# One block for mixing and output: first loads spread over the mixing, transposes that read V in place

## What is computed

```
xn = layernorm(x)
# branch 1: projection to v and two controls, twice a long causal convolution and a gate, output projection
proj = xn @ in_proj_w + in_proj_b
for i in range(2):
    h = implicit_filter(2048, ...)          # one filter a channel, with an exponential window
    v = fft_conv(v, h) * gated_control(ctrl[i], ...)
attn = v @ out_proj_w + out_proj_b
# branch 2
h = bitlinear(xn, w_fc) + gate * (xn @ v.T @ fast_b.T @ u.T)
ffn = bitlinear(relu(h) ** 2, w_proj)
return x + attn + ffn
```

## Time and profile before

| | |
|---|---|
| runs of the kernel, median (lowest to highest) | 952.39 us (951.21 to 956.0) |
| the profiled execution: its time, its span | 950.16 us, 948.6 us |
| TensorE matmul, busy share of the span | 90% |
| TensorE weight load | 76% |
| VectorE, ScalarE, GpSimd | 67%, 50%, 26% |
| moved by DMA | 152.84 MB, mean 161 GB/s |
| granted TensorE clock, mean | 0.963 |

### The profile page before, as it was taken

How to read it: one execution, slowest core, us unless ns; L and a number is a source line. 1 busy time by engine, 2 the same in 40 slices (tenths; PEclk the granted TensorE clock), 3 DMA queues, 4 the chain that set the end, 5 groups by cost and what they waited for, 6 DMA issues and landing times.

```text
span 948.6 us, 26467 instructions
## 1 busy us (share of the span) xinstructions
PE 858.3 (90%) x9972; PEld 716.5 (76%) x9973; DVE 633.6 (67%) x1025; ACT 478.9 (50%) x678; POOL 250.1 (26%) x267
## 2 busy tenths in 40 slices
PE   6836999999999964999999999999999999993995
PEld 3325878888888853888888888888888888873885
DVE  6973898998989972455556565555656556553885
ACT  6413777777777772344443443434334344334761
POOL 1023665646646501111121121211112112110111
PEclk9968999999999996999999999999999999995999
DMA  5373224233242138676778868777777777696797
GB/s 180 105 233 130 94 89 170 97 122 143 88 155 111 73 108 283 123 174 155 166 144 195 182 154 170 148 178 174 171 156 159 177 167 166 125 191 145 241 337 264
DMA packets 86705, 152.84 MB, mean 161 GB/s; under 512 B 12981, under 2 KB 62278, under 8 KB 85382
## 3 DMA queue, kind: packets, MB, share of 16 engines
q1 hardware_dynamic: 74902, 109.01, 47.6%
q0 software_dynamic: 11472, 41.69, 13.4%
q10 hardware_dynamic: 288, 1.57, 0.5%
HBM read 102.83 MB, written 49.41 MB: 160 GB/s over the span
## 4 chain that ended last, share of the span: by engine, by line
PE 47%; DVE 4%; DMA 4%; issue 3%; ACT 2%; SPq 0%; ACTq 0%; POOL 0%; POOLq 0%; DVEq 0%
PE py L1081 14%; PE pp L1062 13%; PE pf L410 6%; PE pf L411 6%; PE pf L412 6%; DVE r L959 2%; DMA Tmid<-filters 1%; DVE r_lo L964 1%; DMA xf_hbm<-xb 1%; DMA GC<-xf_hbm 1%; DMA out<-GC 1%; PE po L410 1%; PE pyT L1273 1%; ACT yg_hi L1207 1%; PE po L411 1%
## 5 line engine op out<-in xcount | busy, mean ns | idle before, releaser
L1081 PEld LDWEIGHTS py<-vwin,lead 64*64 64x64 f32 x5120 | 134.2, 134 | 36.6 <-issue 36.6
L1011 ACT ACTIVATE r_hi<-r 128x512 fp32r<-128x512 f32 x128 | 80.8, 631 | 159.8 <-DVE r L959 159.8
L1081 PE MATMUL py<-vwin,lead 64*64 64x128 f32 (+4 forms) x5120 | 148.1, 266 | 13.7 <-issue 13.5
L964 DVE TENSOR_TENSOR r_lo<-r,r_hi 128x512 fp32r<-128x512 f32 x128 | 101.5, 793 | 78.8 <-ACT r_hi L1011 78.8
L1008 ACT ACTIVATE r<-pf 128x512 f32<-128x512 f32 x128 | 76.6, 598 | 131.9 <-PE pf L412 126.9
L1062 PE MATMUL pp<-wproj,r_hi 128*128 128x256 f32 x512 | 135.7, 298 | 3.6 <-DVE r_lo L964 1.9
L1062 PE MATMUL pp<-wproj,r_lo 128*128 128x256 f32 x512 | 127.2, 281 | 0.0
L451 POOL TENSOR_SCALAR lead<-lead,norms 128x256 f32<-128x256 f32 x64 | 115.3, 1813 | 3.4 <-POOL norms L445 3.4
L1062 PEld LDWEIGHTS pp<-wproj,r_hi 128*128 128x128 f32 x512 | 96.7, 189 | 20.1 <-DVE r_lo L964 6.1
L611 DVE SCALAR_TENSOR_TENSOR xc<-ctrl,taps,xc 128x512 f32<-128x512 f32 x128 | 97.2, 778 | 18.8 <-ACT xc L683 18.1
L959 DVE TENSOR_TENSOR r<-r 128x512 f32<-128x512 f32 x128 | 101.6, 794 | 4.9 <-ACT r L1008 0.6
(11 more groups left out here) (158 smaller groups left out, 1602.7 us busy)
## 6 DMA issues: line engine op xcount, KB each, us to landing
lead<-filters SPq DMA_DIRECT2D x128, 320.0 KB, 6.0
xnT_hbm<-split_b SPq DMA_DIRECT2D x32, 512.0 KB, 3.1
tokens<-xnT_hbm POOLq DMA_DIRECT2D x32, 512.0 KB, 6.9
lead<-in_attn_x SPq DMA_DIRECT2D x16, 512.0 KB, 3.8
gc_hbm<-xc SPq DMA_DIRECT2D x16, 512.0 KB, 2.7
xb<-in_attn_x POOLq DMA_DIRECT2D x16, 512.0 KB, 7.3
GC<-gc_hbm SPq DMA_DIRECT2D x32, 256.0 KB, 7.0
GC<-xf_hbm SPq DMA_DIRECT2D x16, 512.0 KB, 6.7
```

Of the source, the lines that this page charges most:

```text
L964: dve.tensor_tensor(r_lo[j][:, :], r[j][:, :], r_hi[j][:, :].bitcast(F32), ALU.subtract).then_inc(r_split, 1)
L1011: act.activation(r_hi[j][:, :], r[j][:, :], ACT.Copy).then_inc(r_hi_done, 1)
L1081: last = pe.matmul(py[g % 2][q * BW:(q + 1) * BW, side, l, :, A:NB], tile[rows, q * PAIR + l, j * BW:(j + 1) * BW], vwin[g % 2][rows, q, l ...
```

## The change

`output_stage` is gone as a block; its work stands at the end of `mix_stage`, in the same block, without a barrier. Five things change with it:

- The first loads of the output are spread. In order 1, SP's program has its iterations written out; the output weights are loaded after iteration 0, and the gates and the sum of chunks 0 to 3 after iterations 1 to 4. The split of the output weights (`wo_hi`, `wo_lo`) is made within the last iteration of the mixing.
- The transposes read V itself as stationary operand, with a step of 512 bytes from one element to the next. The copies into `ys` are gone, and so are the waits on them.
- The results go to other memory: the transposes to `py`, the output matmuls to `pf` and `pp` in turn, `yg` to a part of GC1's room, the split parts to the feed-forward weights' room, `wo`'s parts to the tokens' room.
- The first two chunks are started between the last feed-forward tiles.
- TensorE's program for the 16 chunks is written out instead of looping.

The core of the diff:

```diff
+                for m in range(ITERS):
+                    body(m, m + ITERS, False)
+                    if m == 0:
+                        sp.wait_ge(y_out, GROUPS // ORDERS + 2)
+                        load_wo(sp)
+                    elif m <= SLOTS:
+                        load_gates(sp, m - 1, m - 1)
+                        sp.wait_ge(xf_saved, 16 * m)
+                        load_sum(sp, m - 1, m - 1)
...
-            sp.wait_ge(y_out, GROUPS // ORDERS + 2)
-            sp.wait_ge(xf_saved, 16 * SLOTS)
-            load_output(sp)
...
+                for c in (SLOTS, SLOTS + 1):
+                    gates(c, c % SLOTS)
+                sp.wait_ge(xf_saved, 16 * (NCH - 1))
...
+            def output(c, j):
+                gated(c, j)
+                summed(c - 2, (j + 2) % SLOTS)
+                yg_low(c, j)
...
+            gated(0, 0)
+            low(NCH - 1, HT - 1)
+            yg_low(0, 0)
+            gated(1, 1)
             scale(NCH - 1)
             add(NCH - 1)
+            yg_low(1, 1)
+            for c in (2, 3):
+                output(c, c)
...
+                    if last and order == ORDERS - 1 and g == 0:
+                        act.wait_ge(wo_in, 16 * KT)
+                        act.wait_ge(fc_mm, (NCH - 1) * HT + HT)
+                        act.activation(wos[0][:, :, :], wo, ACT.Copy).then_inc(wo_hi_ready, 1)
...
+            act.wait_ge(fc_mm, NCH * HT + HT)
+            high(0, 0)
+            high(1, 1)
             act.wait_ge(xf_ready, NCH + 1)
             act.dma_start(xf_hbm[NCH - 1], xb[:, :, :]).then_inc(last_saved, 16)
...
             def transposed(c, j):
                 i = j % 2
-                pe.wait_ge(ys_ready, c + 1)
                 pe.wait_ge(yg_ready, c + 1)
                 for t in range(TB):
-                    last = pe.transpose(pT[i][:, t, :, :].rearrange("p k j -> p (k j)"), ys[i][:, t, :], ident[:, :])
+                    last = pe.transpose(pT[i][:, t, :, :].rearrange("p k j -> p (k j)"), V[:, :, c // CPB, (c % CPB) * TB + t], ident[:, :])
                 last.then_inc(yT_mm, 1)
...
+                pe.wait_ge(y_out, GROUPS + 2)
+                transposed(0, 0)
+                proj(NCH - 1, HT - 2)
+                transposed(1, 1)
+                proj(NCH - 1, HT - 1)
+                pe.wait_ge(wo_split, 1)
+                pe.wait_ge(relu_done, NCH * HT + 2)
+                projected(0, 0)
+                pe.wait_ge(xf_ready, NCH + 1)
+                for c in range(2, NCH):
+                    transposed(c, c % SLOTS)
+                    projected(c - 1, (c - 1) % SLOTS)
+                projected(NCH - 1, (NCH - 1) % SLOTS)
```

More of the change, by code:

```diff
@@ L854, in mix_stage, with lagging @@
         Gs = GC1[:, :, :, :].rearrange("p (b c) n a -> p b c (n a)", b=SIDES)
-        def lagging(eng, order, body):
+        def lagging(eng, order, body, closing=False):
             if order == 0:
                 body(0, 0, True)
-            with eng.Fori(1 - order, ITERS) as m:
+            end = ITERS - (closing and order == ORDERS - 1)
+            with eng.Fori(1 - order, end) as m:
                 body(m, m + ITERS * order, False)
+            if end < ITERS:
+                body(end, end + ITERS * order, False)
         @block.sync
@@ L938, in _ @@
             load_xb(NCH - 1)
+            with pool.Fori(0, NCH // SLOTS) as m:
+                for j in range(SLOTS):
+                    c = m * SLOTS + j
+                    wait_alone(pool, out_ready, c + 3, pool_passed)
+                    pool.dma_start(out_tiles[bass.ds(c, 1)].rearrange("c p i d -> (c p) i d"), xf[j]).then_inc(out_saved[j], 16)
+            for j in range(SLOTS):
+                pool.wait_ge(out_saved[j], 16 * NCH // SLOTS)
         @block.vector
@@ L944, in _ @@
             dve.sem_inc(r_split, 2)
+            dve.sem_inc(yg_ready, 2)
+            dve.sem_inc(out_ready, 2)
+            dve.sem_inc(out_mm, 2)
             dve.wait_ge(srow_in, 16)
@@ L983, in body @@
                     square(it, 2 * g + 1)
-                    low(it, 2 * g + 1)
-            for order in range(ORDERS):
-                lagging(dve, order, lambda m, it, first: body(order, m, it, first))
+                    if last and g == 1:
+                        dve.wait_ge(wo_hi_ready, 1)
+                        dve.tensor_tensor(wos[1][:, :, :], wo, wos[0][:, :, :].bitcast(F32), ALU.subtract).then_inc(wo_split, 1)
+                    if not last or g < GPI - 1:
+                        low(it, 2 * g + 1)
+            for order in range(ORDERS):
+                lagging(dve, order, lambda m, it, first: body(order, m, it, first), True)
+            gated(0, 0)
+            low(NCH - 1, HT - 1)
+            yg_low(0, 0)
+            gated(1, 1)
             scale(NCH - 1)
             add(NCH - 1)
+            yg_low(1, 1)
+            for c in (2, 3):
+                output(c, c)
+            with dve.Fori(1, NCH // SLOTS) as m:
+                for j in range(SLOTS):
+                    output(m * SLOTS + j, j)
+            for c in (NCH - 2, NCH - 1):
+                summed(c, c % SLOTS)
         @block.scalar
@@ L1047, in fc @@
                     tokens = [xm[:, bass.ds(even, 1), part, k, :].rearrange("p s t -> p (s t)") for part in range(2)]
-                    last = split_mm(pe, pf[m % 2][:, :], (wfc[0][:, k, ws], wfc[1][:, k, ws]), tokens, k == 0, k == KT - 1)
+                    last = split_mm(pe, pf[:, m % 2, :], (wfc[0][:, k, ws], wfc[1][:, k, ws]), tokens, k == 0, k == KT - 1)
                     if k == 0 and passed is not None:
```

230 lines of the change are left out of this document (72 added, 158 removed).

## The result

The changed kernel takes 960.25 us (median of 10 runs, 956.87 to 963.2) against 953.76 (10 runs). The ratio of the runs is 1.0054, 95% interval 1.0029 to 1.0079 (the two medians alone would give 1.0068). It is half a per cent slower, where 933 was forecast. The profiled execution spans 957.6 us against 948.6.

The account below looks back on a forecast made before the run. TensorE was taken to bound the mixing, then a hole, then DMA transfers the late output. 18.8 + 0.8 - 1.0 = 18.6 us off 950.16 gave 931.6, or 933.8 on the median, stated as 933; range 927 to 944.

Parts of the forecast that it names:

- The seam: Passage from the mixing's last matmuls to the output's first: closing the hole brings the first store 18.8 us earlier.
- The spread loads: Early gates and sums in the mixing delay T tiles by 1 us in all, taking 165 of 330 GB/s as free.
- After the first store: Rest of the output stage: 0.8 us gained of at most 3.8, as faster engines fill the transfer queues sooner.
- the late pace: Late output stage: full DMA engines at 330 GB/s set 4.77 us a chunk.
- The upper bound that I gave: Mixing: up to 3.2 us of tile delay in each of four iterations, 13 in all.
- The starved tiles: Rival in the mixing: added loads delay T tiles fully, 13 us or more given back, 946 us; chance 0.07.
- the late group: Sign of being wrong: the mixing's last group starts later than 841.8.
- The transposes: Output stage: eight stepped reads from V stay at 1.04 us a chunk, or 2.0 from above; up to 1.8 mostly hidden.
- ScalarE's factor of two: ScalarE's stepped copy takes 2076 ns against 1066 contiguous; basis for the slow transposes rival, 943 us, chance 0.2.
- the two rules weighed: For stepped transposes: SBUF's penalty for each new line, or a weight load of 107 ns whatever the pattern; forecast followed the second.

Follow-up runs that it names:

- e1_late: The changed kernel with gates and sums of chunks 0 to 3 loaded together after the mixing's last tile, as before the change; 945.81 us, 0.9905 of before.
- e9: The changed kernel with late loads, second chunk's tokens held until the second T tile landed, and no sum loads for chunks 4 to 15; 929.52 us.
- e4: The changed kernel with SP's and TensorE's two branches turned back to the order of before; 954.63 us, 0.9983 of before.
- e6: The changed kernel with both the late loads of e1_late and the old branch order of e4; 940.18 us, 0.9829 of before.
- e5: The kernel before with only the order of SP's and TensorE's branches turned round; 959.43 us, 1.0046 of before.

## Why the prediction was wrong

1. **The seam, 18.8 us: right.** Group 63 to the first store fell from 39.2 to 20.6, 18.6 us, and each step (transposes, gate product, low part, output matmuls) stands within 0.2 us of where the text put it. The spread loads had no part in it: e1_late, without them, has 20.4.
2. **After the first store, 0.8 us gained: wrong in sign.** 2.0 us were lost, and over the eight kernels with the new output whole and without copies the stage takes 69.6 to 74.1 us (mean 71.3) against 67.6 and 69.4 with the old. That the transfers set the late pace is right (e9). What I took as a gain, reaching that pace sooner, gives nothing. In all ten kernels with the new output the third store is issued late after an idle time that the profile puts down to "issue" (897.71, some 1.6 us); why, was not tried, and e9 has it too, though VectorE's loop is written out there. The fourth store is back on time, but the seventh chunk's sum can only be loaded behind the third store, into its slot, and the seventh is the next late store in eight of the nine of these kernels that load the sums (in the changed kernel 5.0 us after the sixth; the add ahead of it waited for the sum):

```profile
911.39 1.22 DVE L1040 TENSOR_TENSOR GC<-pf,GC 128x1024 f32<-128x1024 f32 x1 [0.80 <-DMA GC<-xf_hbm]
```

Before, the stores kept their 4.2 us up to the eleventh. That the late third store brings the slow pace on sooner is an inference; no run removes it.
3. **The spread loads, 1 us: the step that failed, 14.7 us in the trace, 14.4 by the medians (e1_late).** The sentence was "On the engines 165 of 330 GB/s are free". The row it cites has the share too, 0.75, and free were 0.25 of the engines' time. T tiles are many small packets: before, from 656 to 679 the trace counts 2340 packets for 3.45 MB (1.5 KB each) at a share of 0.72; in the output, from 890 to 930, 4896 for 13.42 MB (2.7 KB each) at 1.03. By an estimate from these rows 1.05 MB fill the engines for about 3.2 us, and in a quarter of the time that is 13 us to drain, two groups long, with tiles issued in each; in the trace the burst issued at 667.91 had landed at 683.3, 15 us later. The upper bound that I gave, 13 us, was close, but stood in the sum at 1, because I let them drain in 6.4 us at the false rate. The starved tiles, given 0.07, were the case that came: 13.7 us more than the sum had takes the forecast from 933.8 to 947.5, out of its range. With them and without the branches' cost (e4) 954.63 was measured, no gain that can be told from nothing, where that rival had 946. Of the signs of being wrong that the text names, the late group was the true one: the mixing's last group starts at 867.4, not 841.8.
4. **The branches: not in the forecast at all, 5.4 us at the start and 1.1 at group 36.** The full diff, though not the part of it shown above, has `tail > 0` becoming `tail < 1`; I read it as no work moved. By e4 against the changed kernel it is 5.6 us of the median, by e6 against e1 5.6, by e5 against before 4.4 (0.46%). By itself, 6.5 us would have left the time at 940, within the range. An early start was turned into a wait for a tile, behind which the second group's 80 matmuls take 3.96 us instead of 2.28. What the extra microsecond at group 36 is, stays open.
5. **The transposes, 1.04 us forecast with 2.0 as bound: 1.34.** A third of the way. That ScalarE's factor of two was no measure was right. Of the two rules weighed, the penalty for a new line at each access (Advanced Engine Details and Errata, SBUF Cachelines, in the Trainium skill) is borne out in its direction: 256 against 140 ns a load; the rule of the Trainium skill that a load costs its columns alone (TensorE: Matmul & The Clock Gate, LDWEIGHTS), 107 ns here, is not: even the contiguous load takes 140. (The section has a formula in the columns; "whatever the pattern" was my reading of it.) Neither moved the time.
6. **Ahead of the mixing, 5.0 us of the two profiled executions** is not the change's by what the runs show: the code there is the same in all kernels, and the mark lies between 368.4 and 373.7 over twelve of them, at 368.4 in e1_late and 373.7 in the changed kernel. What makes it vary stays open; the medians are over many runs.

The sum of the profiled executions, column by column: 5.0 + 5.4 - 0.6 + 1.1 + 14.7 + 0.1 - 18.6 + 2.0 = 9.1, the difference of the spans (9.0).

## What to carry to other kernels

Free transfer capacity is what the engines' busy share leaves (here 0.25, where the bytes a second next to another stage's peak suggested a half). Loads moved into a stage whose tiles are prefetched one step ahead go in small pieces between the tiles: 0.26 to 0.52 MB a group cost 2 to 4 us in all here, four times 1.05 MB at once 15. And ask first what the move buys: here the seam was as short without it. And compare a stage's first microseconds in both programs: an engine released earlier, even by the order of two branches, issues its loads into other traffic, and the one load it then waits for should go first.

## What the runs showed of the hardware

- With the program that runs in the second branch, SP and TensorE come about 7 us later at the block's start (first matmul 8.4 to 8.8 us after `bo_row`, against 1.3 with the first branch), in three kernels against nine. Where in the branch the time goes, no run shows.
- A stationary operand of 128 fp32 columns read with a step of 512 bytes loads in 256 ns (median 259) instead of 140, and eight transposes in a row take 1.34 us instead of 1.04: of 116 ns more a load 38 show in the pace.
- The granted clock falls in TensorE's wait for a tile: 1.00 up to 682, 0.82 from 682 to 686, where it stands idle, and 0.50, the lower level, for the 4 us after, in which 80 small matmuls take 4.28 us instead of 2.28; over the 23 us with this one wait it is 0.88, and 1.00 in the same stretch before.
- The DMA engines are full at 200 GB/s in the mixing (mean packet 1.6 KB, 667 to 690 of the changed kernel) and at 336 GB/s in the output (2.7 KB, 890 to 930 of before): how many bytes fill them differs by stage.
